# Token blocks of an attention and experts layer: new orders of the same work on four engines of one core

## What is computed

```python
scores = jnp.einsum('bhncd,bhnkd->bhnck', qc, kc) / np.sqrt(D)
scores = jnp.where(causal, scores, -jnp.inf)
intra = jnp.einsum('bhnck,bhnke->bhnce', jax.nn.softmax(scores, axis=-1), vc)
def step(S, inp):
    q_t, k_t, v_t, a_t = inp
    inter_t = jnp.einsum('bhd,bhde->bhe', q_t, S)
    S = a_t[..., None] * S + k_t[..., None] * v_t[..., None, :]
    return (S, inter_t)
```

## Time and profile before

| | |
|---|---|
| median of 3 runs | 4517.09 us (4503.93 to 4520.61) |
| the profiled execution's own time | 4525.55 us |
| its span, first to last instruction | 4523.8 us |
| busy: TensorE, VectorE, ScalarE, GpSimd | 4300.5, 3486.0, 2285.8, 1326.0 us |
| mean granted clock of TensorE | 0.967 |
| token blocks | up to about 3575 us of the span, experts the rest |

### The profile page before, as it was taken

The page is one execution under the profiler, slowest core; times in us unless marked ns, Lnnn a source line. Parts: engine busy times, 40 slices in busy tenths (PEclk is TensorE's granted clock), DMA queues, the critical chain, the costliest instruction groups (busy, mean ns, idle before and its releaser), DMA issues. The chain is left out here.

```text
span 4523.8 us, 182121 instructions
## 1 busy us (share of the span) xinstructions
PE 4300.5 (95%) x73868; PEld 3867.9 (86%) x73868; DVE 3486.0 (77%) x7674; ACT 2285.8 (51%) x7515; POOL 1326.0 (29%) x1266
## 2 busy tenths in 40 slices
PE   5999999999999999999999999999999689999998
PEld 4888888888888888888888888888888579999998
DVE  5777777777777777777777777777777588888887
ACT  4444444444445444444444444545444256666665
POOL 1222222222222222222222222222222156666665
PEclk9999999999999999999999999999999789999999
DMA  2010000000001001001011000110110179999997
GB/s 65 33 36 32 32 32 32 32 32 32 32 32 42 32 32 32 32 32 32 32 37 32 32 32 32 32 32 32 38 37 32 71 235 265 269 265 269 269 265 194
DMA packets 195679, 357.32 MB, mean 79 GB/s; under 512 B 17856, under 2 KB 94016, under 8 KB 194992
## 3 DMA queue, kind: packets, MB, share of 16 engines
q1 hardware_dynamic: 161488, 268.55, 17.7%
q0 software_dynamic: 33632, 79.73, 7.8%
HBM read 242.95 MB, written 107.50 MB: 77 GB/s over the span
## 5 line engine op out<-in xcount | busy, mean ns | idle before, releaser
L473 POOL TENSOR_TENSOR rs<-ve,neg_half 128x1 f32<-128x1 f32 x128 | 78.5, 614 | 2537.1 <-DVE ve L1377 2536.9
L618 ACT ACTIVATE PR<-PR,MX 128x64 f32<-128x64 f32 x2048 | 680.6, 337 | 2.0 <-DVE MX L1336 1.7
L802 PE MATMUL bank<-XBh,wsguh 128*128 128x256 f32 x1536 | 442.0, 288 | 1.5 <-DVE WG L1448 1.5
L626 ACT ACTIVATE OTs<-ot_bank 128x256 f32<-128x256 f32 x256 | 98.4, 384 | 677.6 <-PE ot_bank L960 677.4
L1936 PE MATMUL ebank<-XH,WH 128*128 128x256 f32 x1536 | 430.7, 280 | 7.6 <-DVE XL L2018 7.6
L803 PE MATMUL bank<-XBl,wsguh 128*128 128x256 f32 x1536 | 430.8, 280 | 0.0
L804 PE MATMUL bank<-XBh,wsgul 128*128 128x256 f32 x1536 | 430.8, 280 | 0.0
L1936 PE MATMUL ebank<-XH,WL 128*128 128x256 f32 x1536 | 429.6, 280 | 0.0
L1936 PE MATMUL ebank<-XL,WH 128*128 128x256 f32 x1536 | 429.6, 280 | 0.0
L618 ACT ACTIVATION_READ_ACCUMULATOR PR<-PR,MX 128x1 f32 x2048 | 389.6, 190 | 0.0
L2011 DVE TENSOR_TENSOR WL<-WS,WH 128x768 fp32r<-128x768 f32 (+1 forms) x455 | 370.9, 839 | 16.2
(11 more groups left out here) (231 smaller groups left out, 13341.0 us busy)
## 6 DMA issues: line engine op xcount, KB each, us to landing
WS<-in_L_ffn_w_gate_dram SPq DMA_DIRECT2D x65, 768.0 KB
WS<-in_L_ffn_w_up_dram SPq DMA_DIRECT2D x65, 768.0 KB
WS<-in_L_ffn_w_down_dram SPq DMA_DIRECT2D x65, 768.0 KB
norm_rows<-XR SPq DMA_DIRECT2D x64, 576.0 KB, 3.9
X<-in_L_attn_x_dram SPq DMA_DIRECT2D x64, 512.0 KB, 3.6
out_dram<-X SPq DMA_DIRECT2D x64, 512.0 KB, 5.1
CR<-token_counts,count_at POOLq DMA_INDIRECT x136
XG<-norm_rows,row_at POOLq DMA_INDIRECT x132
```

The source lines that it names most:

```text
L473: nc.gpsimd.tensor_tensor(rs2[:, k:k + 1], ve2[:, k:k + 1], neg_half[:, k:k + 1], ALU.pow).then_inc(rstd2_ready.sem, 1)
L618: ins = nc.scalar.activation(PR[b][:, j, :], PR[b][:, j, :], ACT.Exp, bias=MX[b][:, j:j + 1], scale=1.0, accum_out=SU[b][:, j:j + 1])
L626: nc.scalar.activation(OTs[u // 2][:, 2 * (u % 2):2 * (u % 2) + 2, :], ot_bank[:, 0:2 * P].rearrange("p (a b) -> p a b", a=2), ACT.Copy).t ...
L802: nc.tensor.matmul(out, sh, mh, start=first, stop=False)
```

## The change

It writes `step` anew on TensorE, ScalarE, VectorE and GpSimd, and prologue and epilogue to match, and gives the jobs other banks. The stages themselves, their instructions and the DMA program of SyncE stay as they are. In TensorE's order the three groups outputs(t, 0), scores(t, 3), outputs(t, 1), which stood side by side, are each set between long products; `xt` goes between the two halves of `state_updates`; outputs(0), scores(3) and the first part of k move from the beginning of a step to the end of the one before (their block is called n there, and k's m); `values` is taken in larger pieces. VectorE takes `decays` and `products` a step earlier, ScalarE `gate2`, GpSimd `fold` to `rstd2(0)`. The core of the diff:

```diff
 JOBS = {
-    "Ka": (2, 1), "Kb": (0, 1), "ATr0": (1, 0), "Qb": (3, 1), "V0": (1, 1), "V1": (0, 1), "ATr1": (2, 0), "X2Ta": (3, 0),
-    "X2Tb": (2, 0), "RL": (3, 0), "GU0": (2, 0), "RLT": (3, 0), "KTok0": (0, 1), "KTok1": (0, 1), "GU1": (2, 0), "DK": (0, 1),
-    "GU2": (3, 0), "G1": (2, 2), "Qa": (3, 2), "DN0": (1, 0), "DN1": (3, 0), "G2a": (1, 2), "G2b": (0, 2)}
+    "V0": (1, 1), "ATr0": (0, 0), "Kb": (2, 1), "Qb": (3, 1), "V1": (0, 1), "ATr1": (2, 0), "X2Ta": (3, 0), "X2Tb": (2, 0),
+    "RL": (3, 0), "GU0": (2, 0), "RLT": (0, 0), "KTok0": (1, 1), "KTok1": (0, 1), "GU1": (1, 0), "DK": (0, 1), "GU2": (2, 0),
+    "G1": (1, 2), "Qa": (3, 2), "DN0": (2, 0), "DN1": (1, 0), "G2a": (2, 2), "G2b": (0, 2), "Ka": (0, 2)}
...
@@ GpSimd
             def step(t):
                 n = t.next()
-                fold(t)
-                decayed_k(t)
-                decayed_q(t)
-                rstd1(n)
-                rstd2(t, 0)
-                unpair(n)
+                m = t.next(2)
                 rstd2(t, 1)
+                fold(n)
+                decayed_k(n)
+                decayed_q(n)
+                rstd1(m)
+                rstd2(n, 0)
+                unpair(m)
...
@@ ScalarE
-                q_evac(n, 0)
-                gate2(n, 0)
-                gate2(n, 1)
                 alpha(n)
                 ot(t, 0)
                 exp(t, 2)
+                k_evac(n, 0)
+                q_evac(n, 0)
                 ot(t, 1)
                 exp(t, 3)
                 ot(t, 2)
-                k_evac(n, 0)
                 k_evac(n, 1)
                 ot(t, 3)
                 q_evac(n, 1)
...
                 router_exp(t)
+                hidden_high(t, 0)
                 ktok_evac(n, 1)
                 normalise(m)
-                hidden_high(t, 0)
                 gu(t, 1)
-                exp(n, 0)
                 xt_evac(m, 0)
                 xt_evac(m, 1)
+                exp(n, 0)
                 hidden_high(t, 1)
                 gu(t, 2)
-                hidden_high(t, 2)
                 gate1(m)
                 exp(n, 1)
                 s1_high(m)
+                hidden_high(t, 2)
+                gate2(m, 0)
+                gate2(m, 1)
...
@@ TensorE
-                turn_probs(t, 1)
-                project(n, 0, wk, k_filled, ("Ka", "Kb"), parts=(0,))
-                outputs(t, 0)
-                scores(t, 3)
+                project(n, 0, wk, k_filled, ("Ka", "Kb"), parts=(1,))
                 outputs(t, 1)
-                project(n, 1, wk, k_filled, ("Ka", "Kb"), parts=(0,))
+                values(n, 0, chunks=(0, 1))
                 turn_out(t, 0)
-                project(n, 0, wk, k_filled, ("Ka", "Kb"), parts=(1,))
                 turn_probs(t, 2)
-                project(n, 1, wk, k_filled, ("Ka", "Kb"), parts=(1,))
+                project(n, 1, wk, k_filled, ("Ka", "Kb"))
+                turn_probs(t, 3)
                 outputs(t, 2)
-                turn_probs(t, 3)
                 project(n, 1, wq, q_filled, ("Qa", "Qb"), parts=(0,))
-                values(n, 0, chunks=(0,))
                 outputs(t, 3)
                 values(n, 1, chunks=(0,))
                 turn_out(t, 1)
                 values(n, 1, chunks=(1,))
                 project(n, 1, wq, q_filled, ("Qa", "Qb"), parts=(1,))
-                values(n, 0, chunks=(1, 2))
+                values(n, 0, chunks=(2, 3))
                 x2t(t, 0)
-                values(n, 1, chunks=(2,))
                 x2t(t, 1)
-                values(n, 0, chunks=(3,))
-                values(n, 1, chunks=(3,))
+                values(n, 1, chunks=(2, 3))
                 router_high(t)
                 router_low(t)
                 gate_up(t, 0)
...
                 ktok(n, 1)
                 gate_up(t, 1)
                 state_updates(n, 0)
-                state_updates(n, 1)
                 xt(m, 0)
                 xt(m, 1)
+                state_updates(n, 1)
                 gate_up(t, 2)
                 scores(n, 1)
+                gate1(m)
+                project(m, 0, wq, q_filled, ("Qa", "Qb"))
                 positions(t)
-                gate1(m)
                 turn_probs(n, 0)
-                project(m, 0, wq, q_filled, ("Qa", "Qb"))
                 down(t, 0, (0, 1))
+                scores(n, 2)
                 down(t, 0, (2,))
                 down(t, 1, (0, 1))
-                down(t, 1, (2,))
                 gate2(m, 0)
                 gate2(m, 1)
-                scores(n, 2)
+                outputs(n, 0)
+                down(t, 1, (2,))
+                turn_probs(n, 1)
+                project(m, 0, wk, k_filled, ("Ka", "Kb"), parts=(0,))
+                scores(n, 3)
...
@@ VectorE
-                decays(n)
-                scores_part(t, 3)
-                softmax_b(t, 2)
-                products(n)
                 residual(t, 0)
                 weights(t, 2)
-                decay_part(t, 3)
                 softmax_b(t, 3)
...
+                norm1(m)
                 values(n, 0)
                 values(n, 1)
-                norm1(m)
                 route_a(t)
                 hidden(t, 0)
                 shift1(m)
                 scores_part(n, 0)
+                hidden_low(t, 0)
                 decay_part(n, 0)
                 route_b(t)
-                hidden_low(t, 0)
                 hidden(t, 1)
+                xt_low(m, 0)
                 state(n, (0,))
-                xt_low(m, 0)
                 xt_low(m, 1)
+                state(n, (1, 2))
                 hidden_low(t, 1)
+                scores_part(n, 1)
+                softmax_b(n, 0)
                 hidden(t, 2)
-                softmax_b(n, 0)
-                scores_part(n, 1)
-                state(n, (1, 2, 3))
                 silu1(m)
+                decay_part(n, 1)
+                route_c(t)
+                state(n, (3,))
                 hidden_low(t, 2)
-                route_c(t)
-                decay_part(n, 1)
+                route_rows(t)
+                s1_low(m)
+                total(t, 0)
                 weights(n, 0)
-                total(t, 0)
-                s1_low(m)
                 softmax_b(n, 1)
-                route_rows(t)
+                scores_part(n, 2)
+                decay_part(n, 2)
+                weights(n, 1)
                 total(t, 1)
-                scores_part(n, 2)
-                weights(n, 1)
-                decay_part(n, 2)
+                decays(m)
+                scores_part(n, 3)
+                softmax_b(n, 2)
+                products(m)
+                decay_part(n, 3)
```

More of the change, by code:

```diff
@@ L532, in step @@
                 n = t.next()
-                fold(t)
-                decayed_k(t)
-                decayed_q(t)
-                rstd1(n)
-                rstd2(t, 0)
-                unpair(n)
-                rstd2(t, 1)
+                m = t.next(2)
+                rstd2(t, 1)
+                fold(n)
[4 more added lines that the diff above has]
+                unpair(m)
             rstd1(Turn(0, 0))
             unpair(Turn(0, 0))
+            fold(Turn(0, 0))
+            decayed_k(Turn(0, 0))
+            decayed_q(Turn(0, 0))
+            rstd1(Turn(0, 1))
+            rstd2(Turn(0, 0), 0)
+            unpair(Turn(0, 1))
             with pool.Fori(0, 31) as pair:
@@ L545, in _ @@
                     step(Turn(pair, odd))
-            for odd in range(62, 63):
-                step(Turn(0, odd))
+            rstd2(Turn(0, 62), 1)
             fold(Turn(0, 63))
@@ L1116, in _ @@
             gate2(Turn(0, 0), 1)
[L1117 to L1120, removed]
+            project(Turn(0, 0), 0, wk, k_filled, ("Ka", "Kb"))
+            values(Turn(0, 0), 0, chunks=(0, 1))
+            project(Turn(0, 0), 1, wk, k_filled, ("Ka", "Kb"))
             project(Turn(0, 0), 1, wq, q_filled, ("Qa", "Qb"), parts=(0,))
[L1122 removed]
             values(Turn(0, 0), 1, chunks=(0, 1))
             project(Turn(0, 0), 1, wq, q_filled, ("Qa", "Qb"), parts=(1,))
[L1125 to L1128, removed]
+            values(Turn(0, 0), 0, chunks=(2, 3))
+            values(Turn(0, 0), 1, chunks=(2, 3))
             ktok(Turn(0, 0), 0)
@@ L1132, in _ @@
             state_updates(Turn(0, 0), 0)
-            state_updates(Turn(0, 0), 1)
             xt(Turn(0, 1), 0)
             xt(Turn(0, 1), 1)
+            state_updates(Turn(0, 0), 1)
             scores(Turn(0, 0), 1)
             gate1(Turn(0, 1))
+            project(Turn(0, 1), 0, wq, q_filled, ("Qa", "Qb"))
             turn_probs(Turn(0, 0), 0)
-            project(Turn(0, 1), 0, wq, q_filled, ("Qa", "Qb"))
+            scores(Turn(0, 0), 2)
             gate2(Turn(0, 1), 0)
             gate2(Turn(0, 1), 1)
-            scores(Turn(0, 0), 2)
+            outputs(Turn(0, 0), 0)
+            turn_probs(Turn(0, 0), 1)
+            project(Turn(0, 1), 0, wk, k_filled, ("Ka", "Kb"), parts=(0,))
+            scores(Turn(0, 0), 3)
```

(59 more changed lines are left out.)

37 lines of the change are left out of this document (15 added, 22 removed).

## The result

| | before | after |
|---|---|---|
| median | 4518.85 us (4503.93 to 4527.83, 10 runs) | 4539.85 us (4528.85 to 4556.61, 10 runs) |
| the profiled execution's own time, its span | 4525.55, 4523.8 us | 4543.78, 4542.1 us |
| mean granted clock | 0.967 | 0.974 |
| token block, mean by the router's first line | 54.90 us | 55.31 us |

A forecast was written before the change was run, and what follows sets the result against it. TensorE, busy 95%, was taken as the bound, stalled by code packets behind clustered short products, with low clock following. 126 + 20 - 17 + 16 - 8 = 137 us off 4525.6 gives 4388.6, median 4380; range 4335 to 4465.

The forecast's parts named there:

- Step (5): New orders on the other engines: late answers cost 0.13 us a block, 8 us in all; bounds 0 and 1.0.
- (a): Tight place at the router transposes behind VectorE's last normalise: 0.3 us of room left.
- (b): Tight place at ScalarE's exponentials between evictions of ot_bank: about 4.5 us, covered by 5.1 us of TensorE products.
- (c): Tight place at the gate's bank, now down(0)'s, read by VectorE's total; outputs(0) wants weights(0): some 0.3 us of room.
- Step (1): Opening the cluster outputs(0), scores(3), outputs(1) on TensorE ends stalls for code and the low clock: 126 us less.
- Step (2): Input transposes between the halves of the state products remove 0.33 us of draining a block, 20 us in 62 blocks.
- Step (3): More shape changes on TensorE: three more entries to short products at 0.09 us each, 17 us more in all.
- Step (4): Remaining idle time in the clean block, 0.26 us, are remains of the stall and go too: 16 us.
- three back edges: Blocks where the 16-fold loop turns, 61.14 us each, 8.7 over the clean one; 26 us left uncounted.
- Half: Rival: fetch floor nearer 4 us, or short products set off the low clock; half of (1) stays, 4443 us; 12%.
- no change: Rival: TensorE doesn't wait for code; the second outputs waits for its eviction, then it waits elsewhere; 4514 us; 8%.
- Slower: Rival: ScalarE's exponential chain becomes the bound, its eviction of outputs(1) late; 4616 us if 4.4 us late; 5%.

The follow-up runs named there:

- experiment 1: Changed kernel with only norm1(m) put back behind the two values evictions on VectorE: 4380.36 us, 0.9712 of the kernel before; run again 4379.26 us.
- experiment 2: Changed kernel, order and banks untouched, with norm1's 128x2 addition of EPS made as two 128x1 additions: 4383.16 us, 0.9716 of the kernel before.
- Experiment 5: Changed kernel with norm1(m) behind the values and, on TensorE alone, outputs(0), scores(3), outputs(1) side by side again: 4551.54 us, 1.008 of the kernel before.
- experiment 7: Kernel before with only the 8 input transposes put between the two halves of the state products: 4498.52 us, 0.9978 of the kernel before.
- experiment 3: Changed kernel with only the logits' bank (RLT) put back from 0 to 3: 4419.79 us, 0.9795 of the kernel before.
- experiment 8: Changed kernel with GpSimd's product QD made as two instructions of half the size: 4425.4 us, 0.9815 of the kernel before.
- experiment 6: Changed kernel with norm1(m) behind the values and outputs(1) right behind scores(3), outputs(0) left in its new place: 4446.69 us, 0.9864 of the kernel before.

## Why the prediction was wrong

**Step (5) is the one that failed**, the orders on the other engines, in two ways. Its list of tight places, three with 0.3 to 0.6 us of room, left out the eviction of V1 ahead of `turn_logits`, a place that the diff makes by two edits the prediction named neither of: RLT from bank 3 to bank 0, and `norm1(m)` ahead of the values. And every instruction of VectorE was to be moved at the duration it had where it stood. For L1252 that was 195 ns at the median; moved into QD's time it took 1944. The step was charged 0.13 us a block with a bound of 1.0; removing the wait gives 160 us back (experiments 1 and 2), 2.6 us a block, where 8 us were charged. Of these, 91 us are idle time in the view (60 waits); from the start of the last L810 to that of L1025 it is 101 us more in after than in experiment 1, 1.79 us at the median against 0.12. The other 59 us fit the low clock behind the waits: 158 us at 1.2 GHz in the token blocks of after against 28 in experiment 1, which is worth at most 65. The three places that were named had no waits: L999 for (a), L944 for (b), and the gate's products and L966 for (c) wait for VectorE in no block of after or of experiment 1 apart from the last ones.

**Step (1) held.** The issue waits are gone in after itself, 81 us down to 6. Experiment 5 gives 128 us for the cluster, against 126. This is an indirect value, since in that run ScalarE's waits had to be taken off. The account behind the step closed by luck: it took two of the nine issue lines (45 of 81 us) and the upper bound for the clock (up to 100 us). With all the lines, the same sum would be some 180 us, more than the 152 to be explained, so the low clock was worth less than its bound.

**Step (2) was a little large.** 20 us were put on the drained state products, experiment 7 gives 10 (5 to 14). The self-wait that the trace showed was 16.4 us.

**Step (3) held where it can be seen.** Entering scores from a long product costs 0.21 us, in experiment 1:

```profile
2089.49 0.28 PE L810 MATMUL bank<-XTh,wkl 128*128 128x256 f32 x1
2089.70 0.44 PE L907 MATMUL sa<-QD,RI 32*32 32x64 f32 x32
```

Not the 0.28 or more of an emptied array for each. **Step (4)** has no run of its own; the typical block of experiment 1 is 52.5 us, as forecast.

**The sum.** With the one wait removed the kernel takes 4380.4 and 4379.3 us against a forecast of 4380. That is closer than the steps deserve, and in part luck: 10 us too much in (2) stand against three back edges that the prediction left alone and that fell from 60.0 to 61.1 us to between 54.0 and 56.6, some 16 us together. The sum says nothing for a kernel with the wait in it.

**The rivals.** Half and no change are out: what they name stays (waits for code, waits for the eviction of outputs) is gone in after. *No change* had the second outputs wait for its eviction; in experiment 5 the issue waits come back although ScalarE's order is untouched, and before they fall on a beat of 256 instructions (see the last section), which an eviction doesn't. The Trainium skill, Runtime: NRT & Kernel Launch, section Instruction fetch mechanics, has the fetch hidden; experiments 1 and 5 and the beat contradict it here. *Slower* had the right sign, at 5%, and the right kind (an answer late by an order on another engine, with everything behind it sliding), but the wrong engine and place: ScalarE's exponentials have no wait. The sentence on what would show it wrong named VectorE as the one TensorE would wait for, "by a microsecond a block", through WT, XR or X; it was V.

**What explains the held addition.** First the runs: 128x2 beside a GpSimd product lasts to that product's end (2.15 us), 128x2 beside a product of half the size 0.99, 128x1 in the same place 0.15, 128x2 alone 0.17. The Trainium skill, SBUF — State Buffer, section Who interferes with whom, has a rule for this: VectorE in a mode that uses two ports shares a pair with GpSimd; whoever issues first has it for the whole instruction, and the other waits outright. The runs agree: in after, QD is first in all 62 of its meetings with the addition, by 0.20 us at the median, and the addition ends within 0.03 us of it. The Trainium skill, VectorE: DVE Perf Modes, section Mode 2×_2P — use both read ports for one tensor, lets a single-source operation in SBUF into such a mode if its outermost dimension other than 1 is even, or odd and equal in source and destination. By that, 128x2 enters; of 128x1, which has no such dimension, it doesn't speak, and the runs show only that it isn't held. That it is this lock and no other between the two engines is the rule's word; the runs show only when it holds and for how long.

An even size is not all it takes. `norm2` has a single-source operation too, XR (L1380, 128x512 in SBUF, with two operands read per partition in place of a constant):

```profile
2037.28 0.55 DVE L1380 TENSOR_SCALAR XR<-X,mv,rs 128x512 f32<-128x512 f32 x1 [0.43 <-POOL rs L473]
2037.21 0.24 POOL L502 TENSOR_TENSOR r_mid<-PV,AL 128x16 f32<-128x16 f32 x1
```

It begins in 63 cases of after with 0.18 us of GpSimd's product r_mid to go and takes 0.55 us, as it does in the 65 cases in which no GpSimd instruction is running when it begins. It isn't held. GpSimd's instructions do take longer beside it: rs (L473, 128x1) 0.82 us at the median when it begins while XR runs, 0.54 otherwise. What sets XR apart from the addition no run here varies.

## What to carry to other kernels

Before an instruction is moved on VectorE, look at what GpSimd does at its new place, and take the maximum of its present durations, not the median: an addition of a constant to 128x2 numbers lasted as long as the GpSimd instruction it met, small as it is. Make such a tiny operation as 128x1 ones, or put it behind what others wait for; here either turns a change of +0.5% into -2.9%. Other forms and sizes were not tried. When banks are reassigned, list for every job who empties its bank just before, and price that pair like an edge of the new order.

## What was not expected

- **Size of a wait and the clock.** From 175 us to the last block, after (waits of 1.5 us a block) has 28 stretches at 1.2 GHz, 158 us; with waits of 0.4 to 0.5 us on average (experiments 3 and 8) there are 2 and 3, with none (experiment 1) 3, with the cluster closed 31 (164 us), before 41 (208 us). In all of them TensorE does the same products. Why some blocks of after fall and others, like the one shown at 1.00, don't is open.
- **The gaps before fall on one beat.** Count TensorE's instructions in the order of the trace of before: 56 issue waits are over 0.6 us, and 54 of them come, within two instructions, at one remainder of 256 in each of the loop's three passes (193, 240, 31; it stays at 31 in the epilogue, whose code follows the loop's). The remainder moves by 47 from a pass to the next, and a pass of the loop is 34607 instructions long, which is 47 over a multiple of 256: counted from the start of the loop's code it is one and the same. The two others stand right behind a turn of the loop. The Trainium skill, Runtime: NRT & Kernel Launch, section Instruction fetch mechanics, gives a block of code 256 instructions, and the measured packets fit that. The waits are fixed to places in the program, so the same groups always meet the same boundary; in experiment 5, 42 of 43 such issue waits fall on the same remainders. In experiment 1 three are left, 3.9 us, each right behind a turn of the loop. This is the strongest sign here that code is what the engine waits for.
- **A floor was not measured by itself.** The 3.5 to 3.8 us between packets that the prediction took come from one place; no run here varied only the density of short products, and experiment 6, which was to do it, brought a wait for ScalarE with it.
